# Graph attention over eight batches: VectorE's compares one unit further ahead, the layer norm in front of the negative sums

## What is computed

```python
h  = einsum('bnf,hfo->bhno', x, W)              # B=8, N=2048, F=512, H=8 heads, O=64
s1 = einsum('bhno,ho->bhn', h, a1)
s2 = einsum('bhno,ho->bhn', h, a2)
e  = leaky_relu(s1[..., :, None] + s2[..., None, :], 0.2)
attn = softmax(where(adj > 0, e, -9e15), axis=-1)
out = layernorm(x + (attn @ h).transposed_to(b, n, H*O))
```

## Time and profile before

| | us |
|---|---|
| median of 3 runs | 2936.99 (2936.55 to 2944.32) |
| the profiled execution | 2935.6 |
| its span, first to last instruction | 2933.7 |

### The profile page before, as it was taken

One profiled execution on the slowest core, in us unless ns is written; L12 is line 12 of the kernel. 1 busy time (PEld: TensorE's weight loads), 2 busy tenths in 40 slices (PEclk: granted clock), 3 DMA queues, 4 the chain that ended last, 5 costly groups with the idle time before them and its releaser, 6 DMA issues.

```text
span 2933.7 us, 125924 instructions
## 1 busy us (share of the span) xinstructions
PE 2676.7 (91%) x52546; PEld 2318.7 (79%) x52546; DVE 2580.6 (88%) x3825; ACT 2366.0 (81%) x3950; POOL 823.3 (28%) x1011
## 2 busy tenths in 40 slices
PE   6999989989899898999989989899998999989996
PEld 3698867988579894898948988499884988859886
DVE  6899979998799997999889998899978999889896
ACT  4599964999559994699937998399983999839995
POOL 4522124221342214322152221521216222162221
PEclk9999999999999999999999999999999999999998
DMA  6567643676526754277533775347744477345763
GB/s 173 118 131 172 143 130 73 143 165 140 140 61 162 168 139 118 67 167 172 134 102 80 171 162 129 101 105 170 163 108 115 104 168 171 100 112 123 161 159 99
DMA packets 281205, 390.20 MB, mean 133 GB/s; under 512 B 161856, under 2 KB 161856, under 8 KB 280672
## 3 DMA queue, kind: packets, MB, share of 16 engines
q1 hardware_dynamic: 253536, 315.24, 41.6%
q0 software_dynamic: 27136, 67.12, 13.8%
HBM read 313.52 MB, written 34.14 MB: 119 GB/s over the span
## 4 chain that ended last, share of the span: by engine, by line
PE 31%; DVE 25%; ACT 22%; issue 16%; POOL 2%; DMA 2%; DVEq 1%; ACTq 0%; SPq 0%; POOLq 0%
ACT m_pos L602 20%; PE ps L525 11%; PE ps L556 6%; PE ps L557 6%; DVE m_neg L834 5%; PE ps L496 5%; DVE m_pos L827 3%; DVE m_pos L813 2%; DVE y L698 2%; DVE prod L800 2%; DMA y<-in_x 2%; ACT adj_cut L568 1%; DVE prod_d L803 1%; DVE total L665 1%; PE ps L432 1%
## 5 line engine op out<-in xcount | busy, mean ns | idle before, releaser
L602 ACT ACTIVATE m_pos<-ps,s_steep 128x512 fp8e4<-128x512 f32 x3496 | 2153.4, 1210 | 376.0 <-PE ps L446 281.9
L525 PE MATMUL ps<-b_both,m_pos 128*128 128x130 f16 x16384 | 1026.5, 222 | 113.1 <-DVE total L665 83.7
L525 PEld LDWEIGHTS ps<-b_both,m_pos 128*128 128x128 fp8e5 x16384 | 970.1, 99 | 127.5 <-issue 127.0
L557 PE MATMUL ps<-d_lo,m_neg 128*128 128x65 f16 x16384 | 1035.8, 194 | 24.1 <-issue 23.8
L556 PEld LDWEIGHTS ps<-d_hi,m_neg 128*128 128x128 fp8e5 x16384 | 1017.3, 98 | 37.4 <-issue 37.2
L556 PE MATMUL ps<-d_hi,m_neg 128*128 128x65 f16 x16384 | 1036.0, 193 | 4.0 <-issue 3.7
L557 PEld LDWEIGHTS ps<-d_lo,m_neg 128*128 128x128 fp8e5 x16384 | 1008.3, 98 | 19.4 <-issue 5.7
L827 DVE TENSOR_TENSOR m_pos<-m_pos,maskT 128x1024 uint32<-128x1024 uint32 x512 | 616.7, 1231 | 135.3 <-ACT m_pos L602 104.6
L834 DVE TENSOR_TENSOR m_neg<-m_pos,maskT 128x2048 uint32<-128x2048 uint32 x256 | 583.8, 2280 | 0.3
L496 PE MATMUL ps<-W_sb,xT 128*128 128x512 f32 x1024 | 459.4, 610 | 62.7 <-DVE prod_d L803 60.4
L568 ACT ACTIVATE adj_cut<-adj_in 128x1024 fp8e4<-128x1024 int32 x264 | 397.7, 1577 | 125.9 <-DMA adj_in<-in_adj 125.8
(11 more groups left out here) (95 smaller groups left out, 1606.7 us busy)
## 6 DMA issues: line engine op xcount, KB each, us to landing
adj_in<-in_adj SPq DMA_DIRECT2D x266, 512.0 KB, 4.9
s_bc<-s_rows SPq DMA_DIRECT2D x258, 256.0 KB, 3.8
x_in<-in_x SPq DMA_DIRECT2D x134, 256.0 KB, 4.7
x_sum<-in_x POOLq DMA_DIRECT2D x128, 256.0 KB, 5.8
y<-in_x POOLq DMA_DIRECT2D x32, 1024.0 KB, 9.8
out<-y SPq DMA_DIRECT2D x32, 1024.0 KB, 6.9
maskT<-adj_cut SPq DMA_TRANSPOSE x264, 4.0
m_neg<-in_x SPq DMA_DIRECT2D x10, 256.0 KB, 3.2
```

The source lines that it names most:

```text
L525: mm = pe.matmul(acc, mask, b_both[:, j, h, :, :], start=(j == 0 and it % 2 == 0), stop=(j == JC - 1 and it % 2 == 1))
L557: mm = pe.matmul(acc, mask, d_lo[:, j, h, :], start=False, stop=(j == JC - 1))
L602: ins = nc.scalar.activation(chunk(m_pos[h % 2], j, 0, BLK), ps[:, BANK_S1 + h % 2, :], ACT.Relu, bias=s2_steep[:, j, h:h + 1], scale=STEE ...
```

## The change

1. `compare` is taken out of `make_masks` and called on its own. In the iteration of unit u, VectorE makes the compares of unit u+2 (before: u+1, at the front of the iteration), behind the negative mask, the x maximum, the next batch's preparation and the layer norm, and in front of `take_neg`. It waits for its own negative mask of unit u.
2. `take_neg` moves behind the layer norm and the compares.
3. `turn_s2` moves from the front of unit 31 to unit 30, behind `no_edge_part`; the compares of the next batch's unit 0 follow it there.
4. `dve_slots` gives VectorE other counts. Units 0 to 31, before: 2 3 3 3 3 3 3 3, 3 3 2 1 1 3 3 3, 3 3 2 1 1 3 3 3, 3 3 2 1 1 1 2 1 (75). After: 1 1 2 3 3 3 3 3, 3 3 3 3 2 2 3 3, 3 3 3 3 2 2 3 3, 3 3 3 3 2 2 1 2 (82). ScalarE has the rest of 16 each.

```diff
     def dve_slots(unit):
-        k, h = divmod(max(unit - 1, 0), H)
-        if (k and h in (2, 3)) or unit - 1 in (STAT_UNIT, STAT_UNIT + 2):
+
+        k, h = divmod((unit - 2) % UNITS, H)
+        if unit in (0, 1) or k * H + h == STAT_UNIT:
             return DVE_SLOTS[1]
-        if (k and h == 1) or unit - 1 in (STAT_UNIT + 1, UNITS - 1) or unit == 0:
+        if (k and h in (2, 3)) or k * H + h in (0, STAT_UNIT + 1):
             return DVE_SLOTS[2]
         return DVE_SLOTS[3]
...
             def compare(u, h, nth, unit):
                 hp = h % 2
+                dve.wait_ge(neg_made, at(neg_made, u - 1))
+                dve.sem_inc(waited[dve.engine], 1)
                 dve.wait_ge(s1_loaded[hp], 16 * (nth + 1))
...
-            def make_masks(u, h, mask, nth, unit, first_of_block=None, before=None):
-                compare(u, h, nth, unit)
+            def make_masks(u, h, mask, first_of_block=None, before=None):
                 for qd in range(QUADS):
                     make_pos(u, h, mask, qd, first_of_block)
...
                         with dve.If(b < 1):
-                            make_masks(0, 0, maskT[0], 0, 0, 0)
+                            compare(0, 0, 0, 0)
+                            make_masks(0, 0, maskT[0], 0)
...
                         if unit == UNITS - 1:
-                            turn_s2(b + 1)
-                            dve.sem_inc(waited[dve.engine], 1)
                             with dve.If(b < B - 1):
-                                make_masks(u + 1, 0, maskT[0], (g + 1) * (H // 2), 0, g + 1)
+                                make_masks(u + 1, 0, maskT[0], g + 1)
                             take_pos(u, h)
...
                             no_edge_part(b + 1, 2)
-                        take_neg(u, h, k * IT)
+                            turn_s2(b + 1)
+                            dve.sem_inc(waited[dve.engine], 1)
                         for when, work in ((1, ln_first_half), (2, ln_statistics), (3, ln_apply)):
                             if h == when and k:
                                 work(g - 1, (k - 1) % 2)
+                        if unit < UNITS - 2:
+                            compare(u + 2, (h + 2) % H, g * (H // 2) + (h + 2) // 2, unit + 2)
+                        elif unit == UNITS - 2:
+                            with dve.If(b < B - 1):
+                                compare(u + 2, 0, (g + 1) * (H // 2), 0)
+                        take_neg(u, h, k * IT)
```

More of the change, by code:

```diff
@@ L919, in _ @@
                         if unit == UNITS - 1:
-                            turn_s2(b + 1)
-                            dve.sem_inc(waited[dve.engine], 1)
                             with dve.If(b < B - 1):
-                                make_masks(u + 1, 0, maskT[0], (g + 1) * (H // 2), 0, g + 1)
+                                make_masks(u + 1, 0, maskT[0], g + 1)
                             take_pos(u, h)
                         elif h == H - 1:
-                            make_masks(u + 1, 0, maskT[(k + 1) % 2], (g + 1) * (H // 2), unit + 1, g + 1, before=h)
+                            make_masks(u + 1, 0, maskT[(k + 1) % 2], g + 1, before=h)
                         elif unit > 0:
-                            make_masks(u + 1, h + 1, maskT[k % 2], g * (H // 2) + (h + 1) // 2, unit + 1, before=h)
+                            make_masks(u + 1, h + 1, maskT[k % 2], before=h)
                         else:
```

## The result

| | before | after |
|---|---|---|
| median, us | 2937.89 (2936.55 to 2944.32, 4 runs) | 2896.91 (2894.50 to 2897.61, 4 runs) |
| profiled span, us | 2933.7 | 2892.8 |
| granted clock, mean | 0.976 | 0.977 |

The ratio is 0.984 (95% interval 0.983 to 0.986): 41 us less, where 27 were forecast.

A forecast was written before the change was run, and what follows sets the result against it. ScalarE bounds units 9 to 21, TensorE units 0 to 6 and 21 to 28. Seven turns of 3.3 us, 1.9 in the last batch and 1.6 at the first start make 26.6 us: 2910 us, range 2882 to 2937.

The forecast's parts named there:

- Around the turn: Turn between batches: steep s2 1.0 to 1.1 us sooner, ScalarE's 15th compare of unit 0 costs 0.58; 0.4 us left.
- Batch start: Start of a batch: one VectorE compare instead of three, chunk to chunk 4.46 us becomes 3.4; 1.0 us less.
- First start: Program's first batch start, TensorE far ahead: the whole 1.2 us, and 0.4 for the compare of unit 0; 1.6 us.
- Units 28 to 31: End of a batch: sum of unit 28 2.05 us earlier; 1.9 us a batch gained, bounds 0 and 2.4.
- Units 9 to 21: Middle of a batch: ScalarE's 3.4 us relief given back to the residual wait at unit 17; 0 us, -2 to +2.5.
- rival 1: Unit 17's residual wait does not bind, so ScalarE's 3.4 us come through in eight batches: 2883 us, chance 0.15.
- Rival 2: Units 18 to 21: GpSimd's division and DMA issues held up to 6 us instead of 0.65: 2953 us, chance 0.12.
- Rival 3: Batch end does not move, sum of unit 30 coming when GpSimd is ready: 2925 us, chance 0.20.
- ScalarE's idle time behind unit 19: Sign: ScalarE, before without idle time of note, should idle several us a batch, spread behind unit 19.
- the small multiply: Sign: GpSimd's multiply of 4 columns should be longer than its mean of 363 ns.
- the compares' mean: Sign: the mean time of the compares should fall from 587 ns.
- The wait of the first half: Sign: the layer norm's first half should wait about 50 us for the residual, from 25.7, 5 us at each unit 17.

The follow-up runs named there:

- turn_in_31: The changed kernel with steep s2 and the compare of the next batch's unit 0 back at the front of unit 31: 2901.75 us, ratio 0.986.
- start_three: The changed kernel with 3 compares for unit 1 on VectorE instead of 1, in the batch start: 2890.68 us, ratio 0.983.
- residual_first: The changed kernel with GpSimd issuing the residual DMA in front of the x_sum DMA at unit 16: 2869.52 us, ratio 0.977.
- counts_only: The kernel before, in its old order, with the new 82 compares on VectorE: 2939.66 us, ratio 1.001.
- experiment 4: The changed kernel with the negative sum in front of the compares again in unit 15 alone: 2881.74 us, ratio 0.982.
- order_only: The changed kernel's order with the 75 VectorE compares of before: 2919.93 us, ratio 0.993.
- neg_first: The changed kernel with the negative sum in front of the compares everywhere, behind the layer norm: 2918.48 us, ratio 0.993.
- experiment 2: The run of residual_first, the changed kernel with the residual DMA issued before the x_sum DMA at unit 16: 2869.52 us.

## Why the prediction was right, and where it was not

- **Around the turn**, 0.4 us less: steep s2 came 1.02 us sooner and ScalarE's 15th compare cost 0.62. Measured 0.40. Right, both terms.
- **Batch start**, 1.0: 14.76 to 13.73. Right; turn_in_31 and start_three show that it hangs on unit 1 alone. Chunks 0 to 3 took back 0.34 us a batch, which was not in the sum and which residual_first and counts_only don't show; single batches scatter there from 8.0 to 9.5 us, so this is not clear of noise.
- **First start**, 1.6: 1.67. That it agrees so well is luck. The start of chunk 0, which no edit reaches, lies anywhere from 61.8 to 65.3 us and came 0.55 us later in the changed kernel. From chunk 0 to the first sums it is 50.06 us instead of 52.28: 2.2 us less (50.0 to 50.2 in the six other kernels with this start). The term was a quarter too small.
- **Units 28 to 31**, 1.9: the sum of unit 28 comes 4.08 us behind TensorE's start of the unit instead of 6.20, 2.1 sooner (2.05 forecast); the maxima only 1.73, because the gap in `score_maxima` is 0.38 longer than it was; and from the maxima to the sum of unit 30 it took 0.34 more (0.15 forecast): 1.39. Mechanism right, the sum a third too large. The negative mask can hold GpSimd's reduction, 2.40 us instead of 0.42 in the changed kernel's batch 1:

```profile
730.30 2.40 POOL L991 PARTITION_ALL_REDUCE stat_all<-stat  x1 [11.01 <-issue]
```

```profile
1437.32 0.42 POOL L991 PARTITION_ALL_REDUCE stat_all<-stat  x1 [10.63 <-issue]
```

 But the mask held the reduction in 1 of 8 batches only, where before it was 5 of 8 (the earlier trace rows is a batch without it), and the reduction ended 0.5 us sooner behind the maxima on average. What ate this and more is the division of unit 28: 1.52 us on average from its start to its end, and 0.90 before. It now meets a mask of unit 31. In batch 3, before and after, with that mask:

```profile
1468.53 0.61 POOL L997 TENSOR_TENSOR y<-total,den_scaled 128x256 f32<-128x256 f32 x1
```

```profile
1445.21 1.22 DVE L830 TENSOR_TENSOR m_pos<-m_pos,maskT 128x1024 uint32<-128x1024 uint32 x1 [0.98 <-ACT m_pos L603]
```

```profile
1445.42 1.49 POOL L1005 TENSOR_TENSOR y<-total,den_scaled 128x256 f32<-128x256 f32 x1
```

- **Units 9 to 21**, 0 forecast, 1.70 measured: the step that failed. Of its terms, measured from ScalarE's end of unit 9: the negative sum of unit 15 earlier by 1.2 (1.3 forecast), the division held for 0.73 (0.65) and the DMA issue behind it 0.1 later still, the operations behind the landing 1.3 more (1.2, the 1.8 less what the old order lost), units 19 to 21 quicker by 0.8 (0.5). All held within 0.3. The term that was mis-sized is the x_sum DMA, taken as fixed in length: it landed 4.72 us behind its issue and not 6.85, 2.13 less. So the residual landed 2.6 us sooner and not 0.65. With the two kernels' lag of TensorE behind ScalarE at unit 9 (0.33) that is the 1.70. Why the DMA was shorter stays open (experiment 4). "The DMA in front and the landing are of fixed length" was the sentence that I had put against rival 1, and it was false for the first half; rival 1's mechanism came half true and its time (2883) was missed by 14 us on the one side as the forecast was by 13 on the other.
- **Rival 2**, the wait takes it all: the held division was right in kind and size at the one place, so only 0.73 us and not 6. **Rival 3**, the sum of unit 30 stays: no, 1.39 of 1.9 came.
- **Not forecast:** 0.5 us a batch in units 0 to 9 and 0.4 in units 21 to 28. order_only has the first too (74.10), counts_only not (75.03): it goes with the order. Why is open.
- **What I had named as signs:** the prediction had said that it is wrong if units 9 to 21 take clearly less or more time than before. They took 1.70 us a batch less, so by its own sign it failed there, though the total lies in its range; that range reached down to 2882 because of rival 1. Of the other signs, ScalarE's idle time behind unit 19, the small multiply, the compares' mean, 4.2 us to the sum of unit 28 (4.08) and one compare at the batch start all came. The wait of the first half came to 35.1 us instead of 50 for the reason above.

## What to carry to other kernels

Where an in-order engine waits for a transfer, first ask which of its own earlier transfers stands in front of it on the queue: swapping two DMA issues was worth 20 us here in the stretch that it touches, half as much as the whole change. Moving work off the bounding engine paid only together with an order in which the engine behind it, VectorE, no longer waited and no longer shared its time with GpSimd: the counts alone gave nothing, the order alone 16 us, both 41. And don't price a DMA as fixed when the edit moves its issue against other traffic: bound it from its shortest and longest landing in the trace.

## What the runs showed of the hardware

- **A two-input mask on VectorE holds GpSimd for its length.** A multiply of 4 columns takes 0.20 us beside compares and 1.25 beside a mask of 1.23 us. The Trainium skill, "SBUF — State Buffer", section "SBUF: two separate sides", says that a VectorE operation with two SBUF inputs takes the shared port pair against a GpSimd one that reads SBUF, and the trace agrees (mean 1006 ns after, 205 ns in neg_first). The other way round the compares, with one such input, took 1.65 instead of 1.27 us for three beside the division; by what they were slowed there these runs don't show.
- **The residual DMA is not issued before the x_sum DMA in front of it has landed.** Its issue came 0.38 us behind that landing in all eight batches, before and after, though the program has no wait for it there (`residual` waits for the division alone). Not every GpSimd DMA waits so: in residual_first the x_sum DMA went out 0.87 us behind the residual (959.77 behind 958.90, experiment 2), long before that landed. But it took 12.1 us on average and landed 2.1 us behind the residual, so the x_sum DMA of unit 18, which by the program waits for it, came later. Why only the one order holds the issue is open.
- **TensorE's clock follows these waits.** Four stretches of batch 2 after (columns as in the earlier trace rows), around VectorE's wait for the residual, which ended at 977.6:

```profile
965.00:974.50 9.50, 8.86 (x216) 8.64 (x214) 8.53 (x12) 9.50 (x20) 3.96 (x4) 1.00 0.96 210
974.50:983.50 9.00, 6.56 (x170) 6.35 (x167) 5.80 (x11) 9.00 (x19) 2.24 (x2) 1.00 0.88 204
983.60:990.30 6.70, 5.82 (x57) 5.85 (x58) 6.33 (x14) 6.22 (x11) 2.20 (x3) 0.50 0.58 120
990.50:1003.90 13.40, 13.04 (x342) 12.71 (x339) 13.28 (x20) 12.21 (x21) 6.17 (x5) 1.00 0.50 127
```

 TensorE idled 2.4 of 9 us, and behind that its granted clock was 0.50, the 1.2 GHz level, for 6.7 us. Before and after, such a stretch stands in units 9 to 21 of 6 of 8 batches each, in residual_first in none. In all, the lower level lasted 138.5 us of the span before, 130.9 after and 97.4 in residual_first. Most of what the wait costs is not the clock: the two batches of the changed kernel without such a stretch still took 110.48 and 109.60 us from unit 9 to unit 21, where residual_first takes 108.45, and the mean of all eight is 110.97.
